# Transposing gh and half of z by 32x32 blocks on VectorE and SBUF transfers in place of TensorE

## What is computed

```python
base = x @ W.T
logits = x @ Wr.T + 5 * one_hot(ids)
gates = softmax over the two largest logits, zero elsewhere
y = base + 2 * einsum(einsum(x, A) * gates, B)
out = x + y @ (U * S @ V.T).T
```

## Time and profile before

| | us |
|---|---|
| time, median of 3 runs | 154.13 |
| time of the profiled execution | 153.88 |
| its span | 152.1 |
| TensorE busy | 147.3 |
| VectorE busy | 107.3 |
| GpSimd busy | 72.4 |
| ScalarE busy | 63.6 |

### The profile page before, as it was taken

One profiled execution on the slowest core, in us unless ns is written; L12 is line 12 of the kernel. 1 busy time (PEld: TensorE's weight loads), 2 busy tenths in 40 slices (PEclk: granted clock), 3 DMA queues, 4 the chain that ended last, 5 costly groups with the idle time before them and its releaser, 6 DMA issues.

```text
span 152.1 us, 2911 instructions
## 1 busy us (share of the span) xinstructions
PE 147.3 (97%) x1056; PEld 139.0 (91%) x1056; DVE 107.3 (71%) x297; ACT 63.6 (42%) x141; POOL 72.4 (48%) x57
## 2 busy tenths in 40 slices
PE   7899999999999999999999999999999999999991
PEld 5699999999999989998999899999999998998880
DVE  0787895769578999978755875596558736795851
ACT  4768867884637423346113612351334105013000
POOL 2000433992660659292966276646655640721800
PEclk9999999999999999999999999999999999999999
DMA  5999999999203040059629903980582067006184
GB/s 170 370 401 409 399 410 409 408 406 410 93 4 138 0 138 4 0 222 350 255 87 351 380 15 154 343 332 5 222 234 100 0 278 260 20 0 276 69 340 142
DMA packets 10669, 32.72 MB, mean 215 GB/s; under 512 B 1440, under 2 KB 1952, under 8 KB 10528
## 3 DMA queue, kind: packets, MB, share of 16 engines
q1 hardware_dynamic: 10368, 31.96, 56.0%
q10 hardware_dynamic: 288, 0.59, 1.0%
HBM read 24.16 MB, written 8.39 MB: 214 GB/s over the span
## 4 chain that ended last, share of the span: by engine, by line
PE 93%; DMA 3%; DVE 1%; ACT 0%; SPq 0%; issue 0%; DVEq 0%
PE fin L343 14%; PE fin L345 13%; PE fin L344 13%; PE pj L344 10%; PE pj L343 10%; PE pj L345 10%; PE zt L343 6%; PE zt L345 6%; PE zt L344 6%; DMA w_raw<-in_W 3%; PE gt L427 1%; PE zt L414 1%; PE gt L344 1%; PE gt L345 1%; PE gt L343 1%; DVE w_lo L722 0%
## 5 line engine op out<-in xcount | busy, mean ns | idle before, releaser
L281 POOL TENSOR_TENSOR xT_lo<-xt_raw,xT_hi 128x1024 fp32r<-128x1024 f32 x15 | 36.6, 2441 | 25.2 <-DVE gh L779 7.9
L304 POOL TENSOR_TENSOR x_all<-x_all,vw_raw 128x512 f32<-128x512 f32 x21 | 26.6, 1298 | 25.8 <-DVE vw_raw L827 25.8
L343 PE MATMUL pj<-proj_hi,xT_hi 128*128 128x264 f32 x128 | 36.9, 288 | 0.0
L344 PE MATMUL pj<-proj_lo,xT_hi 128*128 128x264 f32 x128 | 36.3, 284 | 0.0
L345 PE MATMUL pj<-proj_hi,xT_lo 128*128 128x264 f32 x128 | 36.2, 283 | 0.0
L343 PE MATMUL fin<-v_hi,w_hi 128*128 128x256 f32 (+1 forms) x88 | 28.0, 319 | 0.4 <-DVE w_lo L722 0.4
L344 PE MATMUL fin<-v_lo,w_hi 128*128 128x256 f32 (+1 forms) x88 | 27.9, 317 | 0.0
L345 PE MATMUL fin<-v_hi,w_lo 128*128 128x256 f32 (+1 forms) x88 | 27.9, 317 | 0.0
L344 PEld LDWEIGHTS pj<-proj_lo,xT_hi 128*128 128x128 f32 x128 | 24.1, 189 | 0.2
L343 PEld LDWEIGHTS pj<-proj_hi,xT_hi 128*128 128x128 f32 x128 | 24.1, 188 | 0.2
L345 PEld LDWEIGHTS pj<-proj_hi,xT_lo 128*128 128x128 f32 x128 | 24.0, 188 | 0.0
(11 more groups left out here) (94 smaller groups left out, 275.1 us busy)
## 6 DMA issues: line engine op xcount, KB each, us to landing
xt_raw<-in_xt SPq DMA_DIRECT2D x16, 512.0 KB, 6.9
x_all<-in_x SPq DMA_DIRECT2D x16, 512.0 KB, 6.2
out<-x_all SPq DMA_DIRECT2D x13, 512.0 KB, 2.9
vw_raw<-in_VW SPq DMA_DIRECT2D x6, 384.0 KB, 7.4
w_raw<-in_W SPq DMA_DIRECT2D x8, 256.0 KB, 6.5
out<-x_all SPq DMA_DIRECT2D x5, 256.0 KB, 2.0
w_raw<-in_U SPq DMA_DIRECT2D x1, 1024.0 KB, 8.7
aw_raw<-in_AW SPq DMA_DIRECT2D x1, 544.0 KB, 7.6
```

Of the source, the lines that this page charges most:

```text
L281: nc.gpsimd.tensor_sub(xT_lo[:, t % XTR, :, :], xt_raw[:, t % XTR, :, :], xT_hi[:, t % XTR, :, :].bitcast(F32)).then_inc(xt_lo, 1)
L304: nc.gpsimd.tensor_add(x_all[:, t % XR, cols], x_all[:, t % XR, cols], ups[:, j, :]).then_inc(side_add, 1)
L343: nc.tensor.matmul(dst, l_hi, r_hi, start=first, stop=False, skip_group_check=shared)
L344: nc.tensor.matmul(dst, l_hi, r_lo, start=False, stop=False, skip_group_check=shared)
```

## The change

For pairs 1 to 6, TensorE makes no transpose any more. VectorE transposes z's first half of each tile (`turn_z`, between the two parts of the gates) and `gh` of the pair (`turn_gh`) in blocks of 32x32, each in its own place, into `blk`. The blocks then move to their places in `tr`: the four diagonal ones, for `gh` and z of both tiles at once, by four copies of ScalarE on 32 partitions (`move_diagonal`), the six below the diagonal by six transfers issued by SyncE (`move_lower`), the six above it by six issued by ScalarE (`move_upper`). One transfer takes one block of each of the four matrices: 32 partitions with four runs of 128 bytes. ScalarE's copies and transfers of pair p stand ahead of its `split_x(2p+4)`.

`split_gh_moved` reads `tr`. Since z's transpose is no longer added in PSUM, `sums` adds it in, and writes z's first part too; ScalarE copies the second half (`copy_half`), and `split_zb` takes seven blocks of 128 columns (before five, and `split_za` two). `mix(p-1)` moves from `project(2p)` to `project(2p+1)`. `zt` alternates between two banks, `zt` and `gt`. `p1` waits for `zb_lo`. Pairs 0 and 7 keep the transposes on TensorE. `zs`, `blk` and `tr` lie in memory that held W and U. VectorE's list gets a new order.

```diff
+        zs = w_flat[:, 0:8 * P].rearrange("p (j n) -> p j n", n=P)
+        blk = w_flat[:, 8 * P:16 * P].rearrange("p (q m n) -> p q m n", q=2, m=4)
+        tr = w_flat[:, 16 * P:24 * P].rearrange("p (q m n) -> p q m n", q=2, m=4)
...
         zt = bank("zt")
-        gt_both = gt[:, 0:2 * P]
         bv_ps = gt[:, RANK:2 * RANK]
-        zt_v = zt[:, :].rearrange("p (m t n) -> p m t n", m=MC, t=2)
+        zt_bank = [zt, gt]
+        zt_v = [b[:, :].rearrange("p (m t n) -> p m t n", m=MC, t=2) for b in zt_bank]
...
+            def move_lower(p):
+                sp.wait_ge(blk_done, 3 * p)
+                for i in range(SQS):
+                    for j in range(i):
+                        sp.dma_start(tr[SQ * j:SQ * (j + 1), p % 2, :, SQ * i:SQ * (i + 1)],
+                                     blk[SQ * i:SQ * (i + 1), p % 2, :, SQ * j:SQ * (j + 1)]).then_inc(tr_load, 16)
...
+                if p < PAIRS - 1:
+                    move_lower(p)
                 if p >= 2:
                     store_pair(p - 2)
...
-                    if t >= 2 and t % 2 == 0 and k == MH:
+                    if t == 2 and k == MH:
+                        mix(0)
+                    if t >= 5 and t % 2 == 1 and k == MH:
                         mix(t // 2 - 1)
...
+                    if k == MH + 1 and (p == 0 or p == PAIRS - 1):
+                        pe.wait_ge(z_copied, 2 if p == 0 else 4)
                         for t in range(2):
-                            nc.tensor.matmul(zt_v[:, 0, t, :], z_sb[:, t, :], ident[:, :], start=False, stop=False,
+                            nc.tensor.matmul(zt_v[p % 2][:, 0, t, :], z_sb[:, t, :], ident[:, :], start=False, stop=False,
                                              is_transpose=True, skip_group_check=True)
                 last.then_inc(xt_used, 1)
...
             def zt_free(p):
-                pe.wait_ge(za_lo, p)
-                pe.wait_ge(sums_done, 4 * p)
+                if p == 1:
+                    pe.wait_ge(bv_lo_done, 1)
+                if p == 2:
+                    pe.wait_ge(za_lo, 1)
+                if p >= 2:
+                    pe.wait_ge(sums_done, 4 * (p - 1))
+                if p >= 3:
+                    pe.wait_ge(z_half_copied, p - 2)
...
-                    pe.wait_ge(gt_lo, p)
                 for t in range(2):
-                    last = nc.tensor.transpose(gt[:, t * P:(t + 1) * P], gh[:, t, :], ident[:, :])
+                    last = nc.tensor.transpose(dst[:, t * P:(t + 1) * P], gh[:, t, :], ident[:, :])
                 last.then_inc(gt_done, 1)
...
-                    last = triple(zt[:, 2 * m * P:2 * (m + 1) * P], bv_hi[:, cols], bv_lo[:, cols],
+                    last = triple(zt_bank[p % 2][:, 2 * m * P:2 * (m + 1) * P], bv_hi[:, cols], bv_lo[:, cols],
...
-                pe.wait_ge(za_lo, p + 1)
                 if p == 0:
+                    pe.wait_ge(za_lo, 1)
                     pe.wait_ge(us_lo_done, 1)
+                else:
+                    pe.wait_ge(zb_lo, p + 1)
                 free_bank(p, 4)
                 product(p, bank_a, 0, *us(0, 0), True, False)
 
             def p6(p):
-                pe.wait_ge(zb_lo, p + 1)
                 if p == 0:
+                    pe.wait_ge(zb_lo, 1)
...
-                transpose_gh(p)
+            transpose_gh(PAIRS - 1)
...
+            def copy_half(p):
+                act.wait_ge(zt_done, p + 1)
+                act.wait_ge(zb_lo, p)
+                nc.scalar.copy(zs[:, 1:3, :], zt_v[p % 2][:, 1, :, :]).then_inc(z_half_copied, 1)
 
             def split_zb(p):
                 act.wait_ge(sums_done, 4 * p + 4)
-                nc.scalar.copy(zh[:, p % 2, 2:7, :], zs[:, :, :]).then_inc(zb_hi, 1)
+                if p == 0:
+                    nc.scalar.copy(zh[:, 0, 2:7, :], zs[:, 2:7, :]).then_inc(zb_hi, 1)
+                else:
+                    zh_free(p)
+                    nc.scalar.copy(zh[:, p % 2, :, :], zs[:, 0:7, :]).then_inc(zb_hi, 1)
+
+            def split_gh_moved(p):
+                act.wait_ge(tr_load, MOVES * p)
+                act.wait_ge(tr_diag, SQS * p)
+                nc.scalar.copy(ghT_hi[:, :], tr[:, p % 2, 0:2, :]).then_inc(gt_hi, 1)
+
+            def move_diagonal(p):
+                act.wait_ge(blk_done, 3 * p)
+                for i in range(SQS):
+                    rows = slice(SQ * i, SQ * (i + 1))
+                    nc.scalar.copy(tr[rows, p % 2, :, rows], blk[rows, p % 2, :, rows]).then_inc(tr_diag, 1)
+
+            def move_upper(p):
+                for i in range(SQS):
+                    for j in range(i + 1, SQS):
+                        act.dma_start(tr[SQ * j:SQ * (j + 1), p % 2, :, SQ * i:SQ * (i + 1)],
+                                      blk[SQ * i:SQ * (i + 1), p % 2, :, SQ * j:SQ * (j + 1)]).then_inc(tr_load, 16)
...
             def pair(p):
                 if p < PAIRS - 1:
                     split_x(2 * p + 2)
-                split_za(p - 1)
-                copy_x22(p - 1)
                 copy_u(p - 2)
-                copy_z(2 * p)
+                if p == 2:
+                    split_gh_moved(1)
+                if p == PAIRS - 1:
+                    copy_z(2 * p)
                 exp_top(2 * p)
-                split_zb(p - 1)
                 if p < PAIRS - 1:
                     split_x(2 * p + 3)
-                copy_z(2 * p + 1)
+                if p >= 3:
+                    split_gh_moved(p - 1)
+                copy_half(p - 1)
+                split_zb(p - 1)
+                if p == PAIRS - 1:
+                    copy_z(2 * p + 1)
                 exp_top(2 * p + 1)
-                split_gh(p)
+                if p < PAIRS - 1:
+                    move_diagonal(p)
+                    move_upper(p)
+                else:
+                    split_gh(p)
...
+            move_diagonal(1)
+            move_upper(1)
             split_x(5)
-            split_gh(1)
...
+            def turn_z(t):
+                nc.vector.transpose(blk[:, (t // 2) % 2, 2 + t % 2, :], pj[t % 2][:, Z0:TCOLS]).then_inc(blk_done, 1)
+
+            def turn_gh(p):
+                dve.wait_ge(gh_done, 2 * p + 2)
+                nc.vector.transpose(blk[:, p % 2, 0:2, :], gh[:, :, :]).then_inc(blk_done, 1)
...
+            def split_gh_moved(p):
+                dve.wait_ge(gt_hi, p + 1)
+                nc.vector.tensor_sub(ghT_lo[:, :].rearrange("p (t n) -> p t n", t=2), tr[:, p % 2, 0:2, :],
+                                     ghT_hi[:, :].bitcast(F32).rearrange("p (t n) -> p t n", t=2)).then_inc(gt_lo, 1)
...
             def sums(p):
                 n = 4 * p
-                nc.vector.tensor_add(zs[:, 1, :], zt_v[:, 0, 1, :], zs[:, 0, :]).then_inc(sums_done, 1)
+                dve.wait_ge(zt_done, p + 1)
+                dve.wait_ge(tr_load, MOVES * p)
+                dve.wait_ge(tr_diag, SQS * p)
+                dve.wait_ge(z_half_copied, p)
+                nc.vector.tensor_add(zs[:, 0:8:7, :], zt_v[p % 2][:, 0, :, :], tr[:, p % 2, 2:4, :]).then_inc(z0_done, 1)
+                dve.wait_ge(z0_done, p)
+                nc.vector.tensor_add(zs[:, 3, :], zs[:, 7, :], zs[:, 2, :]).then_inc(sums_done, 1)
                 dve.wait_ge(sums_done, n + 1)
-                nc.vector.tensor_sub(zs[:, 2, :], zs[:, 1, :], zt_v[:, 0, 0, :]).then_inc(sums_done, 1)
+                nc.vector.tensor_sub(zs[:, 4, :], zs[:, 3, :], zs[:, 0, :]).then_inc(sums_done, 1)
                 dve.wait_ge(sums_done, n + 2)
-                nc.vector.tensor_sub(zs[:, 3, :], zs[:, 0, :], zs[:, 2, :]).then_inc(sums_done, 1)
-                nc.vector.tensor_sub(zs[:, 4, :], zt_v[:, 1, 0, :], zs[:, 2, :]).then_inc(sums_done, 1)
+                nc.vector.tensor_sub(zs[:, 5, :], zs[:, 2, :], zs[:, 4, :]).then_inc(sums_done, 1)
+                nc.vector.tensor_sub(zs[:, 6, :], zs[:, 1, :], zs[:, 4, :]).then_inc(sums_done, 1)
 
             def split_zb(p):
                 dve.wait_ge(zb_hi, p + 1)
-                nc.vector.tensor_sub(zl[:, p % 2, 2:7, :], zs[:, :, :],
-                                     zh[:, p % 2, 2:7, :].bitcast(F32)).then_inc(zb_lo, 1)
+                first = 2 if p == 0 else 0
+                nc.vector.tensor_sub(zl[:, p % 2, first:7, :], zs[:, first:7, :],
+                                     zh[:, p % 2, first:7, :].bitcast(F32)).then_inc(zb_lo, 1)
...
+            def gates(t):
+                gates_top(t)
+                if 2 <= t < TILES - 2:
+                    turn_z(t)
+                gates_apply(t)
+
             def pair_2():
                 split_zb(0)
                 split_us(1)
-                split_za(1)
                 up(0, 1)
                 up(0, 2)
+                split_gh_moved(1)
                 xb1(0)
+                gates(4)
                 sums(1)
-                gates_top(4)
-                gates_apply(4)
-                gates_top(5)
-                gates_apply(5)
+                gates(5)
+                turn_gh(2)
                 xa0(0)
```

(86 more changed lines are left out.)

16 lines of the change are left out of this document (5 added, 11 removed).

## The result

The changed kernel takes **168.94 us** (166.88 to 169.6) beside 154.19 for the kernel before on the same chip: a ratio of 1.09, interval 1.0862 to 1.0938; the ratio leaves out the two slowest of the six runs, 169.54 and 169.6. It is slower, and close to the forecast of 167.6. The profiled execution took 166.88 us with a span of 165.0 us, 12.9 more than before.

What follows compares the result with a forecast made beforehand. TensorE bounded the old kernel; after the change a 16.65 us chain over the other engines sets each pair's pace. Losses of 16.15 less 2.64 give +13.5 us, 167.6 by the median, range 151.2 to 176.

Steps and rivals of the forecast that it cites:

- T: End of `turn_gh(p)` on VectorE, from which each pair's later steps are placed; the next T foreseen 16.65 us later.
- GpSimd's piece: GpSimd's part of splitting tile 2p+4, starting 0.08 us behind ScalarE's `split_x` and taking 2.42 us.
- The sum: Losses over all pairs: 2.4 + 5.2 + 7.5 + 0.4 + 0.65 = 16.15 us, less 2.64, gives +13.5.
- The steady pair, TensorE's side: TensorE's 14.14 us of work plus waits of 0.4 at `p1` and 2.1 at `mix` make 16.65.
- The removed transposes: Pairs 1 to 6 lose four TensorE transposes each, 24 x 0.11 = 2.64 us; a pair needs 14.14.
- The issues: ScalarE's six transfer issues at 0.47 us each, 2.8 us, delay its `split_x` to T + 3.75.
- The lock on `pick`: VectorE's `pick`, both inputs in SBUF, is ready at T + 5.6 but waits for GpSimd until T + 7.30.
- The lock by the additions: GpSimd's three additions, 1.28 us each, hold `split_gh_moved` until after the first and the sums until after the third.
- The queues keep up: Rival: issues cost ScalarE next to nothing or the lock is weaker, the chain fits 14.14, 151.5 us; chance 0.18.
- Half a lock: Rival: `pick` slips through, only `split_gh_moved` and sums wait; chain 14.96, 156.4 us; chance 0.10, shared with somewhat shorter chains.
- The transfers land late: Rival: small block transfers land near T + 10 or later, 170 to 192 us; chance 0.12 above 173, shared with dear issues.

Runs made afterwards that it cites:

- short piece: Changed kernel with GpSimd subtracting only one of eight chunks of tiles 6 to 15, ScalarE's issues kept: 159.11 us, ratio 1.0329.
- both causes away: Changed kernel with no transfers issued by ScalarE and GpSimd subtracting one of eight chunks of tiles 6 to 15: 152.41 us, ratio 0.9872.
- the repeat: The changed kernel measured again with no edit, as base for other runs on the same chip: 168.32 us, ratio 1.0907.

## Why the prediction was right, by its steps

| step | predicted | measured |
|---|---|---|
| T(1), T(2) | 50.1, 69.2 | 50.08, 68.66 |
| one issue on ScalarE | 0.47 | 0.62 median (0.595 to 1.51) |
| ScalarE free behind T | 3.7 | 4.89 (T(3)) |
| GpSimd's piece | T + 4.88 to 7.30 | T + 6.02 to 8.41 |
| `pick` ends with it, `gh` | 7.97 | 9.02 |
| `up` twice | 9.39 | 10.45 |
| `split_gh_moved` | 10.42 | 11.24 |
| TensorE's wait at `mix` | 2.1 | 0.56 the first, 2.07 the others |
| TensorE's wait at `p1` in a steady pair | 0.4 | none |
| sums | 14.0 | 14.64 |
| next T | 16.65 | 17.16; the others 16.55 |
| whole | +13.5 | +12.9 in the span |

(Places behind T are those of the pair at T(3) = 85.22, in which one issue took 1.51 us; in the pairs of 16.55 us ScalarE is free some 0.6 us earlier.)

**The sum.** Over 14.14 us the first interval cost 4.44, the next four 2.42 + 3.02 + 2.41 + 2.41 = 10.26, and the last, from T(6) = 135.48 to the transposes at 150.51, 0.89; with 0.1 at T(1) that is 15.7, less 2.64: 13.0 at that point, and 12.9 in the span. The forecast had 16.15: 0.5 more for the first, 0.2 less for the four, 0.16 more for pair 7 and the tail.

**The steady pair, TensorE's side.** The pace came out (16.65 foreseen, 16.55 or 16.56 measured in three of the five intervals), although one of TensorE's terms was not there. I had 14.14 + 0.4 at `p1` + 2.1 at `mix`. `split_zb` ended at 105.33, T + 2.95, and `p1` began at 105.57 without a wait. In place of the 0.4 stand the 0.34 us that the wait at `mix` costs in busy time. The chain over the other engines sets the pace, so TensorE had to lose 2.4 us a pair in one way or another; that its wait at `mix` alone came so near the 2.1 is luck. At the start of the changed pairs `p2(0)` waited 1.31 us for `copy_u` (foreseen 0.95), and the second wait for it, 0.41, was not foreseen.

**The removed transposes.** Right: with all waits away a pair takes 14.15 us, by the sum 14.14.

**The issues.** The step was right, two terms were mis-sized. I took 0.47 from ScalarE's two loads; a transfer between two SBUF places held the queue for 0.62 us in the median, and one for 1.51 (at 85.89): with the gaps six took 4.75 us there and some 4.1 in the other pairs, not 2.8. The diagonal copies, for which I had added 0.9, run beside the issues and cost ScalarE's stretch nothing. So it became 4.3 to 4.9 instead of 3.7 (4.1 in the first pair). The pace came out at 16.55 all the same because the steps further on were together some 0.7 us shorter than foreseen, 0.4 of it at `split_gh_moved` and the sums. The total was hit in part by errors that cancel: the 4 us that I had set on an issue of 0.6 do not show in it, though the issue did cost 0.62, as the copies' 0.9 and the 0.7 further on take them back.

**The lock on `pick`.** Right, and the middle of the case: 1.71 us in place of 0.15, to the end of GpSimd's piece. The short piece takes 8.9 us off the kernel, and the pair goes from 16.55 to 15.0 us, by what `pick` no longer loses. It also shortens `split_zb` (1.07 us instead of 1.86), for which TensorE was not waiting in a steady pair.

**The lock by the additions.** Half right. I let `split_gh_moved` wait for the first addition and the sums for all three. It took 0.88 instead of 0.42 and ended 0.79 behind `up`, foreseen 1.03; of the sums only one was stretched, to 0.52 instead of 0.28, and they were over 1.41 us after the first, foreseen 2.0.

**The rivals.** *The queues keep up* failed at its own condition: 0.60 and not 0.07 us for an issue. But its price was wrong too. With no issues at all it should have been 151.5, and it was 156.81: an earlier piece of GpSimd locks `dtop`, `split_zb` and `split_gh_moved` instead of `pick`. I had asked only whether `pick` is hit, and had taken `dtop`, one input of 2 columns with one number a partition to subtract, for free; it took 1.09 us. The Trainium skill, "SBUF — State Buffer", section "Who interferes with whom", names `tensor_scalar` among the operations that can take the shared ports in one of its fast modes. The row fits that; whether `dtop` ran in such a mode no run shows. The 151.5 belongs to both causes away, 152.41. *Half a lock*, 156.4, assumed that `pick` slips through; it did not. *The transfers land late* did not happen in the changed kernel: queue q10 moved 5184 packets more, 144 for each transfer, in 3.2% of 16 x 165.0 us less 1.0% of 16 x 152.1: 60 us, or 0.012 each, not 0.084. The 78% that the prediction takes from the Trainium skill, "DMA: Bandwidth & Descriptors", section "Why small descriptors are slow (HBM only)", is given there for a 1 MB remote transfer, as a share of the link's rate. Here these packets moved 0.59 MB in the 60 us, some 10 bytes a ns, beside some 23 on queue q1 (32.55 MB in 54.0% of 16 x 165.0 us): less than half the rate of the large transfers, and still early enough. It is no idle rival, though: with the same transfers at another moment they gave 196.74 us, beyond the 192 that I had set as its end.

**What I had not priced.** The granted clock can fall when TensorE waits: 0.88 over 28 us in the repeat. The first profile shows none of it, with the same waits of 2 us, and its own time, 166.88, is what the steps should be held against: they gave 167.4. The median of 168.94 has a part beyond them, which the forecast lacked and its surplus of 0.5 us covers only in part. What decides which run sees it stays open.
